# Attention of a decoder layer on one core: a low half and one copy moved one head earlier, and the fourth scores of the 128-column tile put between the 384-column tile's spread and its values

## The reference

```python
def attn(x, Wq, Wk, Wv, Wo):                    # x is (4, 512, 512), 16 heads of 32
    q, k, v = (x @ Wq), (x @ Wk), (x @ Wv)      # each reshaped to (B, T, H, Dh)
    scores = einsum('bthd,bshd->bhts', q, k)
    scores = scores * tril(ones((T, T)))        # masked scores are 0, not -inf
    attn = softmax(scores / T ** 0.5, axis=-1)
    return einsum('bhts,bshd->bthd', attn, v).reshape(B, T, H * Dh) @ Wo

x = x + attn(layernorm(x), ...)
x = x + xattn(layernorm(x), ctx, ...)           # a single-head attention over a context
x = x + ffn(layernorm(x), ...)                  # 4-bit weights, 512 -> 4096 -> 512, tanh gelu
```

## Time and profile before

| | |
|---|---|
| median of 3 runs | 1457.94 us (1457.32 to 1458.15) |
| the profiled execution's own time | 1456.45 us |
| span of that execution, first to last instruction | 1454.7 us |
| TensorE busy | 97% |
| VectorE, ScalarE, GpSimd busy | 68%, 48%, 27% |
| granted TensorE clock | 1.0 throughout |

### The profile page before, as it was taken

The page is one execution under the profiler, slowest core; times in us unless marked ns, Lnnn a source line. Parts: engine busy times, 40 slices in busy tenths (PEclk is TensorE's granted clock), DMA queues, the critical chain, the costliest instruction groups (busy, mean ns, idle before and its releaser), DMA issues.

```text
span 1454.7 us, 26922 instructions
## 1 busy us (share of the span) xinstructions
PE 1414.1 (97%) x8896; PEld 719.3 (49%) x8896; DVE 989.0 (68%) x2125; ACT 699.1 (48%) x1600; POOL 388.4 (27%) x705
## 2 busy tenths in 40 slices
PE   6999999999999999999999999999999999999999
PEld 3475467457546744444444444444444444444444
DVE  7796688589578868886665675666666666766533
ACT  5794288149428834435335344353353353443432
POOL 1054234305473455421211121221112112212100
PEclk9999999999999999999999999999999999999999
DMA  7563613542455501010100100100001001000011
GB/s 253 135 187 111 183 63 96 144 122 88 148 153 186 203 19 44 17 34 17 33 18 17 34 17 17 33 16 20 17 17 34 17 17 34 17 17 1 1 59 58
DMA packets 77311, 98.02 MB, mean 67 GB/s; under 512 B 8049, under 2 KB 60785, under 8 KB 76785
## 3 DMA queue, kind: packets, MB, share of 16 engines
q1 hardware_dynamic: 77168, 96.23, 21.5%
HBM read 68.94 MB, written 27.26 MB: 66 GB/s over the span
## 4 chain that ended last, share of the span: by engine, by line
PE 86%; DVE 4%; ACT 4%; issue 4%; POOL 1%; DMA 0%; ACTq 0%; DVEq 0%; POOLq 0%; SPq 0%
PE bank L901 25%; PE bank L903 25%; PE bank L902 25%; PE bank L968 3%; ACT prob L1290 2%; PE bank L989 2%; PE bank L956 1%; PE bank L914 1%; PE bank L1044 1%; PE bank L1029 1%; PE bank L998 1%; PE bank L1039 1%; DVE xt L1606 1%; PE bank L1050 1%; DMA X<-in_x_dram 0%
## 5 line engine op out<-in xcount | busy, mean ns | idle before, releaser
L901 PE MATMUL bank<-xs,G 128*128 128x512 f16 x896 | 339.8, 379 | 2.4 <-issue 1.1
L902 PE MATMUL bank<-xs,G 128*128 128x512 f16 x896 | 339.6, 379 | 0.0
L903 PE MATMUL bank<-xs,G 128*128 128x512 f16 x896 | 339.6, 379 | 0.0
L1752 DVE TENSOR_TENSOR c<-bank,c 128x512 f32<-128x512 f32 x128 | 88.0, 689 | 193.6 <-PE bank L903 193.6
L1368 ACT COPY c<-bank 128x512 f32<-128x512 f32 x192 | 111.2, 579 | 220.9 <-PE bank L903 216.0
L901 PE MATMUL bank<-Wd,hid 128*128 128x512 f16 x512 | 194.1, 379 | 2.8 <-DVE X L1806 2.8
L903 PE MATMUL bank<-Wd,hid 128*128 128x512 f16 x512 | 194.0, 379 | 0.0
L902 PE MATMUL bank<-Wd,hid 128*128 128x512 f16 x512 | 194.0, 379 | 0.0
L764 POOL TENSOR_TENSOR c<-c,m 128x512 f32<-128x512 f32 x64 | 82.3, 1286 | 389.4 <-ACT c L1368 389.4
L1806 DVE SCALAR_TENSOR_TENSOR X<-bank,col,X 128x512 f32<-128x512 f32 x128 | 95.4, 750 | 101.5 <-PE bank L903 101.4
L1290 ACT ACTIVATE prob<-bank,nmx 128x129 f32<-128x129 f32 (+3 forms) x256 | 146.9, 586 | 8.4 <-POOL nmx L779 8.4
(11 more groups left out here) (197 smaller groups left out, 2391.5 us busy)
## 6 DMA issues: line engine op xcount, KB each, us to landing
stack<-qk_dram SPq DMA_DIRECT2D x128, 128.0 KB, 3.3
sc_in<-scale_t SPq DMA_DIRECT2D x30, 384.0 KB
qk_dram<-qk SPq DMA_DIRECT2D x32, 256.0 KB, 3.0
packed_t<-pk_t SPq DMA_DIRECT2D x32, 192.0 KB, 1.9
pk_in<-packed_t SPq DMA_DIRECT2D x30, 192.0 KB
X<-in_x_dram SPq DMA_DIRECT2D x4, 1024.0 KB, 5.7
pk_in<-L_ffn_gate_W_packed_dram SPq DMA_DIRECT2D x16, 256.0 KB, 2.7
pk_in<-n_L_ffn_up_W_packed_dram SPq DMA_DIRECT2D x16, 256.0 KB, 3.1
```

The costliest lines, as they stand in the source:

```text
L901: pe.matmul(o, lhs(0), rhs(0), start=first, stop=False, skip_group_check=onto)
L902: pe.matmul(o, lhs(0), rhs(1), start=False, stop=False, skip_group_check=onto)
L903: return pe.matmul(o, lhs(1), rhs(0), start=False, stop=stop, skip_group_check=onto)
L1752: nc.vector.tensor_tensor(dst[:], bank[at][:], dst[:], ALU.add).then_inc(comb, 1)
```

## The change

Three edits, no instruction added or taken away.

```diff
@@ GpSimd, body @@
                         if j > 0 and i > 1:
                             convert(n * (NB // B) + r, r, 3 * i + j - 7)
-                        if j == 3 and i == 0 and r > 1:
+                        if j == 2 and i == 0 and r > 1:
                             out_tail(n, r - 2)
@@ TensorE, body @@
                         if u + 1 < UNITS:
                             scores(n, u + 1, j)
+                        if j == 3 and u > 0 and sooner(u - 1):
+                            values(n, u - 1)
                         turn(n, u, j)
...
                         if j == 2 and u > 0 and sooner(u - 1):
                             recips(n, u - 1)
-                            values(n, u - 1)
@@ ScalarE, body @@
                             exp(n, u, j)
-                        if j == 3 and u % TT < 2:
+                        if j == 3 and u % TT == 0:
                             turned(n, u, 0)
                             turned(n, u, 1)
-                        elif j >= 2 and u % TT >= 2:
+                        elif j >= 2 and u % TT > 0:
                             turned(n, u, j - 2)
```

## The result

| | before | changed |
|---|---|---|
| median of 19 runs | 1458.15 us (1456.49 to 1460.38) | 1460.85 us (1458.67 to 1463.64) |
| ratio, 95% interval | | 1.002 (1.0014 to 1.0026) |
| span of the profiled execution | 1454.7 us | 1461.6 us |

The changed kernel is 2.7 us slower. The forecast was 0.4 us faster, with a range that ended at 1459.8; the measured time lies above it.

A forecast was written before the change was run, and what follows sets the result against it. TensorE, busy 97% of the span, was taken as the bound, so only its waits could be won. Per batch 0.10 - 0.10 - 0.10, times 4, gave -0.4 us: 1457.94 to 1457.5 us, range 1454.8 to 1459.8.

The forecast's parts named there:

- wait of the fourth scores: TensorE, 12 places: unit 8's fourth scores, moved before the values, wait 0.25 us for unit 7's fourth exp.
- turn of unit 7's last head: TensorE's transposes of that head's probabilities, queued behind the values: start at 95.14, not 94.86, 0.28 us late.
- first exp of unit 9: ScalarE, first exp of the 256-column unit: stays near 97.2, since its shift no longer waits for GpSimd's low half.
- repack's second half waits: TensorE at unit 9: its 0.34 us wait for ScalarE's first copy goes, second half starts 0.31 earlier.
- next spread: TensorE turning reciprocals into rows, after VectorE's copy of the repack: that copy comes 0.10 us earlier behind unit 7.
- group 2: Attention stretch from unit 7's first exp to unit 11's: 0.10 us shorter; group 3 the same.
- group 1: Attention stretch from unit 3's first exp to unit 7's, without a low half: 0.10 us longer.
- the 0.10 behind the scores: TensorE: after a wait for an exp, the values start 0.10 us behind the fourth scores, read from 92.90 to 93.00.
- who is late next: With the repack's wait gone, VectorE's copy of its second half sets the pace: starts 100.21, 0.10 us earlier than 100.31.
- the canceling: GpSimd's low half, one head earlier at 8 places, cancels the 0.28 us delay for ScalarE at unit 9's first exp.
- the first: Rival, chance 0.09: new wait is carried to the end, unit 9's first-head copy does not pay; +3.4, 1461.3 us.
- three signs by which the forecast would be wrong: Groups 2 and 3 change by more than 0.3, the repack still waits, or a stretch outside attention changes length.

The follow-up runs named there:

- e5: Changed kernel with the fourth scores between the values' product with V and its extra-column part: 1459.14 us against 1457.07 before, ratio 1.0009.
- e4: Kernel before with only the ScalarE copy edit and the GpSimd low-half edit, no TensorE edit: 1456.04 us, ratio 0.9992.
- e7: e4 with VectorE's copy of the repack moved before the small sum of the last unit: 1455.73 us against 1457.07 before, ratio 0.9989.
- e8: Changed kernel with VectorE's copy of the repack moved before the small sum of the last unit: 1460.62 us, ratio 1.0025 against before.
- e3: Kernel before with only the GpSimd edit, low half behind the third shift at units 8 and 12: 1455.51 us, ratio 0.9989.
- e2: Kernel before with only the ScalarE edit, copy of the first turned head before the fourth exp: 1456.98 us, ratio 0.9996.
- e6: Changed kernel with the fourth scores moved further forward, in front of the spread: 1464.27 us against 1457.07 before, ratio 1.0052.

## Why the prediction was wrong

Its steps, at the place of unit 7, all lined up on the read-out of the fourth exp; "late" is against before:

| step | forecast | measured |
|---|---|---|
| wait of the fourth scores | 0.25 | 0.25 |
| values behind the scores (start to start) | 0.10 | 0.21 |
| turn of unit 7's last head | 0.28 late | 0.41 late |
| third turn of unit 8 | 0.28 late | 98.21-1.40-96.34 = 0.47 late |
| spread of unit 7 | 0.19 late | 98.66-1.40-96.91 = 0.35 late |
| first exp of unit 9 | not late | 0.24 late |
| repack's second half waits | no | no |
| next spread | 0.10 early | 102.50-1.40-100.97 = 0.13 late |
| group 2 | -0.10 | +0.14 |
| group 1 | +0.10 | +0.37 |

**The step that failed first is the 0.10 behind the scores.** The forecast looked at the right place, but took what it saw there for the price of a wait, and from the wrong rows: 92.90 to 93.00 is a turn behind scores, both 128 wide. The step needed a 32-wide instruction behind a 128-wide one. The trace of the kernel before had its price at two places, the idle of the weight loads at 93.56 and at 94.79, but it was read as part of the work. Two more changes of width cost 0.16 up to the turn on top of the 0.25, and 0.22 with the turn's own slower start. At 12 places, 0.2 of extra delay is 2.4 us. That the 0.25 itself came out was in part luck: it was worked out as a wait for the exp alone, and some 0.11 of it would be there without one (e5).

The Trainium skill's rule was weighed there (TensorE: Matmul & The Clock Gate, Step-by-step: what each phase is for: weight loads are pulled ahead of matmuls in flight when the row groups do not conflict or the load goes to the background weight buffer) and said to be worth 0.4 us less. For equal widths the loads above agree with it, 0.06 and 0.11 ahead of their products. Between widths they come ahead by 0.03 at most, and this is where the 0.16 lies.

**The second is who is late next.** VectorE's copy was thought free 0.61 behind the start of its second maximum, with the small sum that stands between them left out; with the repack out of the way it stands 0.69 behind it, in the changed kernel (101.16 to 101.85) as in e4. That alone would have turned the -0.10 into -0.02. But e7 and e8 show that the copy is not even what binds. The sum followed ScalarE through the first copy and exp 3 and stopped there, asking only whether the scores would need that exp; the second copy behind it, which the third turn needs, was the one to follow. Moving a copy in front of an exp had taken the wait from the repack's second half and put a shorter one on the turn behind it.

**The third is the canceling.** The low half's move was to cancel the 0.28 by which unit 9's first exp would be late. It removes 0.22 (e3: groups 2 and 3 0.21 shorter), and with the maximum 0.47 late, not 0.28, 0.24 remain. Behind unit 3, where no low half helps, the whole 0.47 reaches the exp, and the copy edit gives a part back: group 1 pays 0.37.

**What held:** the wait of 0.25 at all 12 places; the low half is free in its new place; the repack's wait goes; unit 1 costs nothing (the stretch in front of the first group is 8.32 to 8.36 in all kernels); nothing outside attention changed by the edit (the first exps of two batches are 126.95 apart before and 127.62 after, which is the longer attention alone, and the 3.2 us that one profiled execution lost behind 510 us have no room in the 2.7 between the medians). Of the rivals, the first was nearest: the delay is carried to the end. Its price was 0.28 a place, 3.4 us, and its ground a copy that does not pay. In truth the copy pays (e2, 0.12 in groups 2 and 3) and the delay that is carried is 0.39. None of the three signs by which the forecast would be wrong appeared: groups 2 and 3 moved by 0.14, under the 0.3 allowed, though not the way that was forecast. The bound of 0.3 a group, 2.4 us over these eight alone, was too wide to tell.

The forecast also put a delay of 0.2 to 0.3 on three engines that were all within 0.2 of each other, added the slack of each and came to zero. With slacks that small, an error of 0.1 at one handover was worth 1.2 us, four tenths of what the forecast called no change.

## What to carry to other kernels

When an instruction is moved on TensorE, count the changes between tile widths in the new order as well as the waits: price them from a place where the same pair of shapes stands back to back, not from any neighbour behind a wait. An early start for an instruction whose operand is late is paid by everything queued behind it. Where three engines run with slacks of 0.2 us, follow each one to its next handover after the place that was improved, and test each small edit alone: here two of three were small gains that the third one hid.

## What the runs showed of the hardware

Between products of equal width the weight load started 0.06 to 0.11 ahead of its product (94.80 to 94.86, 93.69 to 93.80). Where the width changed between 128 and 32 columns it started 0.00 to 0.03 ahead, after an idle of 0.17 to 0.20, or of 0.08 behind the short scores of 129 columns. Those scores were followed by a product of their own width in 0.07 (94.79 to 94.86), and by a 32-wide one in 0.16 (94.74 to 94.90 in e5), 0.17 (96.14 to 96.31 in e6) and 0.21 (95.45 to 95.66 in the changed kernel). Put between two parts of the values, with nothing to wait for, they made the turn behind them 0.23 later than in their old place (e5).

The change between f16 and f32 is not the cause: the scores are f16 and the turn at 94.86 is f32, and at equal width the load between them starts at 94.80, right behind that of 94.79; the turns in front of the spread are f32 like it, and show an idle of 0.17. What in the array holds the load back, no run here shows.
